# A four-stage-pair transformer on Trainium2: the last four heads of the 8-dimension attentions weigh their values in float32

## The reference, cut to what matters

```
for L in (L0, L2):
    q = layernorm(x) @ Wq (+ bq)              # 128 tokens, 16 heads x 8
    k, v = ctx @ Wk (+ bk), ctx @ Wv (+ bv)   # 77 keys, 16 heads x 8
    p = softmax(q k^T / sqrt(8))              # per head, 128 x 77
    x = x + tanh(gate) * ((p v) @ Wo (+ bo))
```

## Time and profile before

| | |
|---|---|
| runs of the kernel before (us) | 5861.38, 5869.38, 5875.85; median 5869.38 |
| the profiled execution: time, span (us) | 5845.47, 5843.6 |
| mean granted TensorE clock | 0.923 |
| PE, PEld, DVE, ACT, POOL busy (us) | 4882.0, 3691.1, 4188.7, 2757.5, 2105.6 |
| first to last `hiT` work, stage L0 (us) | 28.2 to 568.7 |
| the same, stage L2 (us) | 2493.3 to 3033.8 |
| other big stages, `weigh` products (us) | 935.4 to 1660.6, 3551.2 to 4459.6, 4654.0 to 5367.7 |

### The profile page before, as it was taken

How to read it: one execution, slowest core, us unless ns; L and a number is a source line. 1 busy time by engine, 2 the same in 40 slices (tenths; PEclk the granted TensorE clock), 3 DMA queues, 4 the chain that set the end, 5 groups by cost and what they waited for, 6 DMA issues and landing times. The chain is left out here.

```text
span 5843.6 us, 134152 instructions
## 1 busy us (share of the span) xinstructions
PE 4882.0 (84%) x40251; PEld 3691.1 (63%) x40251; DVE 4188.7 (72%) x10467; ACT 2757.5 (47%) x5756; POOL 2105.6 (36%) x2536
## 2 busy tenths in 40 slices
PE   7888998999942996088879998888888799998898
PEld 5666567888842564066657665777776577776544
DVE  7887775777765332288876767888887699997544
ACT  4554674555520332055555544555554355554344
POOL 3332000011037001643333336777776633333300
PEclk9998998999975998599989998999999899998988
DMA  0000500000011343100000000000000000000000
GB/s 33 2 2 21 230 0 16 5 5 5 5 59 43 131 139 102 48 3 2 2 13 1 0 0 9 0 0 0 0 0 6 7 2 2 2 2 6 1 13 16
DMA packets 113844, 136.89 MB, mean 23 GB/s; under 512 B 45016, under 2 KB 88216, under 8 KB 108956
## 3 DMA queue, kind: packets, MB, share of 16 engines
q1 hardware_dynamic: 105504, 118.30, 6.1%
q0 software_dynamic: 8192, 16.79, 1.0%
HBM read 44.85 MB, written 58.72 MB: 18 GB/s over the span
## 5 line engine op out<-in xcount | busy, mean ns | idle before, releaser
L1881 POOL TENSOR_TENSOR l3a_probs<-l3a_probs,l3a_later 128x512 f32<-128x512 f32 x256 | 320.7, 1283 | 4.9 <-DVE l3a_total L2069 4.9
L1867 POOL TENSOR_TENSOR l3a_keys<-l3a_kT,head 128x2048 f32<-128x2048 f32 x64 | 230.5, 3601 | 232.5 <-ACT l3a_kT L1994 232.5
L1296 POOL DMA_INDIRECT l1c_rows<-l_rows,l1f_slots x128 | 122.2, 955 | 443.8 <-PEq L1288 403.3
L359 POOL TENSOR_TENSOR l0x_keys<-l0x_kT,head 128x1232 f32<-128x1232 f32 x64 | 145.1, 2268 | 354.7 <-ACT l0x_kT L446 354.7
L359 POOL TENSOR_TENSOR l2x_keys<-l2x_kT,head 128x1232 f32<-128x1232 f32 x64 | 145.1, 2267 | 321.1 <-ACT l2x_kT L444 321.1
L1929 PE MATMUL l3a_scores<-l3a_keys,l3a_qT 128*128 128x512 f32 x512 | 256.5, 604 | 4.2 <-POOL l3a_keys L1867 4.2
L166 POOL TENSOR_TENSOR l1x_ve<-l1x_mv,eps 128x1 f32<-128x1 f32 x64 | 12.3, 191 | 656.1 <-DVE l1x_mv L158 656.1
L294 PE MATMUL l3a_po<-l3a_vals,l3a_probsT 128*128 128x32 f32 x2048 | 248.1, 269 | 0.1
L294 PEld LDWEIGHTS l3a_po<-l3a_vals,l3a_probsT 128*128 128x128 f32 x2048 | 247.1, 192 | 0.4 <-ACT l3a_probsT L275 0.4
L250 ACT ACTIVATE l3a_probs<-l3a_probs 128x512 f32<-128x512 f32 x256 | 161.7, 632 | 180.5 <-DVE l3a_probs L241 175.5
L1367 POOL TENSOR_TENSOR l2f_hid<-l2f_prod,l2f_route 128x512 f32<-128x512 f32 x128 | 152.2, 1194 | 255.3 <-DVE l2f_prod L1514 242.2
(11 more groups left out here) (520 smaller groups left out, 17315.5 us busy)
## 6 DMA issues: line engine op xcount, KB each, us to landing
l_rows<-l0f_zeros SPq DMA_DIRECT2D x34, 1024.0 KB, 25.9
l1f_parts<-l1f_split SPq DMA_DIRECT2D x40, 512.0 KB, 3.6
l1e_x_in<-l_rows SPq DMA_DIRECT2D x40, 256.0 KB, 2.8
l1f_down<-l1f_w SPq DMA_DIRECT2D x40, 256.0 KB, 2.4
l_rows<-l1e_y_out SPq DMA_DIRECT2D x40, 256.0 KB, 2.7
l1f_w<-in_L_W SPq DMA_DIRECT2D x16, 256.0 KB, 3.2
out_x<-x_res SPq DMA_DIRECT2D x16, 256.0 KB, 2.0
x_res<-in_x SPq DMA_DIRECT2D x1, 3840.0 KB, 12.6
```

The source lines that it names most:

```text
L359: pool.tensor_tensor(keys[it.par][:, :, :], kT[it.par][:, :].unsqueeze(1).to_broadcast([P, HEADS, KEYS]), g.head8[:, :].unsqueeze(2).to_br ...
L1296: pool.indirect_dma_start(rows[p][:, k * P:(k + 1) * P], None, g.xs[:, :], bass.IndirectOffsetOnAxis(ap=slots[:, it.b * CHOICES + k:it.b * ...
L1867: pool.tensor_tensor(keys[it.par][:, :, :, :], kT[it.par][:, :, :].unsqueeze(2).to_broadcast([P, J, G4, T]), g.head32[:, :].unsqueeze(1).u ...
L1881: pool.tensor_tensor(v, v, later[:, :].unsqueeze(1).to_broadcast([P, 4, T]), ALU.mult).then_inc(s_masked, 1)
```

## The change

For the last chunk (heads 12 to 15) of both 8-dimension stages, the turned probabilities are copied to one float32 buffer `wholeT`, the values of these heads to a float32 `vwhole`, and the product is one float32 matmul a head. The other twelve heads keep their three fp16 products. DVE's remainder 3 is dropped; `vhi` and `vlo` hold twelve heads; ACT makes one more small copy, `vwhole`, which `vlo` waits for; fetch 1 and fetch 3 no longer share a buffer, so fetch 3 waits for `weigh3` of the round before and fetch 1 for `weigh1` of it. Scaling by 64 and 1024 falls away for the four heads in numerator and denominator alike (their ones column holds 1.0).

```diff
@@ Softmax
+        if last_whole:
+            self.wholeT = st.sb("wholeT", [keys, CHUNK * P])
...
+        self.rests = self.nc_ - 1 if last_whole else self.nc_
@@ Softmax.turn
-        if (due := nth(it, self.nc_, c, back=2)) is not None:
+        if self.last_whole:
+            if c == 1:
+                if (due := nth(it, self.nc_, self.nc_ - 1, ago=1)) is not None:
+                    pe.wait_ge(self.s_fetch, due)
+            elif (due := nth(it, self.rests, c - 2 if c >= 2 else self.rests - 1, ago=0 if c >= 2 else 1)) is not None:
+                pe.wait_ge(self.s_rest, due)
+        elif (due := nth(it, self.nc_, c, back=2)) is not None:
             pe.wait_ge(self.s_rest if self.split else self.s_fetch, due)
@@ Softmax.fetch
-        if (due := nth(it, self.nc_, c, back=2)) is not None:
+        if (due := nth(it, self.nc_, c, back=4 if self.last_whole and c % 2 else 2)) is not None:
             act.wait_ge(self.s_values, due)
         src = self.ps_turn[c % 2][0:self.keys, :]
-        if self.split:
+        if self.last_whole and c == self.nc_ - 1:
+            act.copy(self.wholeT[:, :], src).then_inc(self.s_fetch, 1)
+        elif self.split:
@@ Softmax.times_values
-        pe.wait_ge(self.s_rest if self.split else self.s_fetch, nth(it, self.nc_, c))
+        whole = self.last_whole and c == self.nc_ - 1
+        if self.split and not whole:
+            pe.wait_ge(self.s_rest, nth(it, self.rests, c))
+        else:
+            pe.wait_ge(self.s_fetch, nth(it, self.nc_, c))
         for k in range(CHUNK):
             h, cols = CHUNK * c + k, slice(k * P, (k + 1) * P)
+            if whole:
+                last = pe.matmul(out_of(h), self.wholeT[:, cols], values_of(h), start=True, stop=True)
+                continue
@@ small_head_attention
+    SPLITS = HEADS - CHUNK
-        vhi, vlo = st.sb2("vhi", [KEYS, HEADS, D + 1], F16), st.sb2("vlo", [KEYS, HEADS, D + 1], F16)
+        vhi, vlo = st.sb2("vhi", [KEYS, SPLITS, D + 1], F16), st.sb2("vlo", [KEYS, SPLITS, D + 1], F16)
+        vwhole = st.sb2("vwhole", [KEYS, CHUNK, D + 1])
...
+                    pool.memset(vwhole[i][:, :, D:D + 1], 1.0).then_inc(s_ones, 1)
...
+                    if c == 3:
+                        pe.wait_ge(s_vwhole, nth(it))
+                        sm.times_values(pe, it, c, lambda h: o_p[:, h, :], lambda h: vwhole[it.par][:, h - SPLITS, :])
...
-                    act.activation(vhi[it.par][:, :, 0:D], v_heads, ACT.Copy, scale=SPLIT).then_inc(s_vhi, 1)
+                    act.activation(vhi[it.par][:, :, 0:D], v_heads[:, 0:SPLITS, :], ACT.Copy, scale=SPLIT).then_inc(s_vhi, 1)
+                    act.copy(vwhole[it.par][:, :, 0:D], v_heads[:, SPLITS:HEADS, :]).then_inc(s_vwhole, 1)
...
                     dve.wait_ge(s_vhi, nth(it))
+                    dve.wait_ge(s_vwhole, nth(it))
...
-                steps = ... "divide remainder0 remainder1 maximum0 normalize maximum1 shift0 remainder2 remainder3 shift1 statistics values maximum2 add shift2"
+                steps = ... "divide remainder0 remainder1 maximum0 normalize maximum1 shift0 remainder2 shift1 statistics values maximum2 add shift2"
```

More of the change, by code:

```diff
@@ L198, with __init__ @@
 class Softmax:
-    def __init__(self, st, g, banks, heads_of_bank, keys, scale, ps_turn, split=False):
+    def __init__(self, st, g, banks, heads_of_bank, keys, scale, ps_turn, split=False, last_whole=False):
         self.g, self.banks, self.keys, self.scale = g, banks, keys, scale
@@ L211, in __init__ @@
         self.mx, self.probs = st.sb2("mx", [P, HEADS]), st.sb2("probs", [P, HEADS, keys])
-        self.split = split
+        self.split, self.last_whole = split, last_whole
+        if last_whole:
+            self.wholeT = st.sb("wholeT", [keys, CHUNK * P])
         if split:
@@ L324, in small_head_attention @@
         ln = LnFront(st, g, pa[:, 0:P])
-        sm = Softmax(st, g, scores, HELD, KEYS, scale, turned, split=True)
-        s_w, s_ctx, s_ones = st.sem("s_w"), st.sem2("s_ctx"), st.sem("s_ones")
+        sm = Softmax(st, g, scores, HELD, KEYS, scale, turned, split=True, last_whole=True)
+        s_w, s_ctx, s_ones, s_vwhole = st.sem("s_w"), st.sem2("s_ctx"), st.sem("s_ones"), st.sem("s_vwhole")
         s_kv, s_q, s_kT, s_vhi, s_vlo, s_qT, s_keys = [st.sem(n) for n in ("s_kv", "s_q", "s_kT", "s_vhi", "s_vlo", "s_qT", "s_keys")]
@@ L413, in weigh @@
                             pe.wait_ge(s_o, due)
-                        pe.wait_ge(s_ones, 4)
-                    sm.times_values(pe, it, c, lambda h: o_p[:, h, :], lambda h: (vhi[it.par][:, h, :], vlo[it.par][:, h, :]))
+                        pe.wait_ge(s_ones, 6)
+                    if c == 3:
+                        pe.wait_ge(s_vwhole, nth(it))
+                        sm.times_values(pe, it, c, lambda h: o_p[:, h, :], lambda h: vwhole[it.par][:, h - SPLITS, :])
+                    else:
+                        sm.times_values(pe, it, c, lambda h: o_p[:, h, :], lambda h: (vhi[it.par][:, h, :], vlo[it.par][:, h, :]))
                 def turn_o(it):
@@ L505, in value_remainder @@
                     dve.wait_ge(s_vhi, nth(it))
-                    dve.scalar_tensor_tensor(vlo[it.par][:, :, 0:D], v_heads, SPLIT, vhi[it.par][:, :, 0:D],
+                    dve.wait_ge(s_vwhole, nth(it))
+                    dve.scalar_tensor_tensor(vlo[it.par][:, :, 0:D], v_heads[:, 0:SPLITS, :], SPLIT, vhi[it.par][:, :, 0:D],
                                              ALU.mult, ALU.subtract).then_inc(s_vlo, 1)
@@ L519, in _ @@
                          "statistics": (statistics, 0), "normalize": (lambda it: ln.normalize(dve, it), 1),
-                         **numbered("remainder", lambda it, c: sm.remainder(dve, it, c), 4, 3),
+                         **numbered("remainder", lambda it, c: sm.remainder(dve, it, c), 3, 3),
                          "values": (value_remainder, 1), "divide": (divide, 4), "add": (add, 4)}
-                skewed(dve, g.B, in_order(steps, "divide remainder0 remainder1 maximum0 normalize maximum1 shift0 remainder2 remainder3 "
+                skewed(dve, g.B, in_order(steps, "divide remainder0 remainder1 maximum0 normalize maximum1 shift0 remainder2 "
                                                  "shift1 statistics values maximum2 add shift2"), 6)
```

## The result

The changed kernel takes 6047.64 us (median of 4 runs, 6038.97 to 6050.22) against 5868.85 us: ratio 1.0303, 95% interval 1.0291 to 1.0316, so 179 us slower. That is 1.40 us for each of 128 rounds. The forecast had 1.02 us and 6000 us; the time lies inside the range.

What follows compares the result with a forecast made beforehand. It took a loop closing on PE (last `weigh`, `vhi`, `vlo`, `queries`) as the bound. Terms 0.64 + 0.05 + 0.33 = 1.02 us a round, times 128 = +131 us, gave 6000 us as a median; range 5930 to 6090.

Steps and rivals of the forecast that it cites:

- (a): Remainder 3 leaves DVE's queue: 0.66 us less DVE work a round, but 0 on the path.
- DVE bound: Rival: DVE's queue holds the loop at `vlo`, so each round shortens by 0.69 us, to 5781 us; chance 0.03.
- (b): `weigh3` on PE: four float32 products replace twelve fp16 ones, 0.64 us more a round, including 0.07 for the first load.
- Four loads a product: Rival: each float32 product in `weigh3` needs four load-and-product pairs, round 2.08 us longer, 6135 us; chance 0.03.
- cheap float32: Rival: the eight float32 records of `weigh3` flow like fp16 ones, leaving 0.05 us a round, 5876 us; chance 0.03.
- (c): Extra ACT copy `vwhole` behind `vhi`, with `vlo` waiting for it: 0.05 us more a round, bounds 0 and 0.15.
- the wait at turn 2: PE's new waits at turns 0 to 3 ask for things done long before: 0 on the path.
- ACT's idle time before `vhi`: Sign in the profile after: ACT's idle time there grows by about 0.6 us a round.
- (e): PE's clock: a longer thin part from `weigh2` to `queries` brings more half-speed stretches, 0.33 us more a round.
- every round hit: Rival: PE's clock falls in each round, 1.56 us a round more, 6069 us; chance 0.12.
- The price of a hit: Extra length of a round hit by a half-speed stretch: 1.30 us, from rounds of 9.37 and 8.07 us.

Runs made afterwards that it cites:

- e1: The changed kernel with DVE's fourth 77x512 conversion a round kept in its old place, its result unread; ratio 1.0307.
- e2: The kernel before with only the extra small ACT copy (77x32, float32, unread) behind `vhi`, and `vlo` waiting for it; ratio 1.0010.
- e12: The kernel before, all fp16 products kept, with an unread 756-column ACT copy behind `vhi` that `vlo` waits for; ratio 1.0356.
- e7: The changed kernel with `weigh2` and `weigh3` issued before `score2` and `output` on PE; ratio 0.9979.
- e10: The changed kernel with the query projection moved to the first score bank and ACT's second exponential put ahead of `fetch_values`; ratio 1.0005.
- e5: The kernel before with the query projection written to the first score bank, so `queries` need not wait for `vlo`; ratio 0.9834.

## Why the prediction was right, and where it was short

The sign, the range and the path of the added work (`weigh3`, `vhi`, `vlo`, `queries`) held; the sum was 0.38 us a round short, nearly all of it in one term, the clock.

(a), DVE's remainder at 0: right, and shown by e1. The rival of the DVE bound is out.

(b), `weigh3` in float32 at 0.64 us: measured 1.04 - 0.45 = 0.59 us. The length 1.02 was near 1.04. The 0.07 us for a first load that couldn't hide was wrong: the first float32 product starts 0.03 us behind the last fp16 one. Four loads a product is out with the eight records, and cheap float32 with their 1.04 us. The Trainium skill's "FP8 and Floating Point Precision", section TensorE Precision Notes, has four passes for true fp32; the profile shows two records for a product, so the passes don't give the cost of this shape. The load price of "TensorE: Matmul & The Clock Gate", section on LDWEIGHTS (128 / 1.2 = 107 ns for 128 columns, by which the prediction's estimate was 0.65 us), gives 0.58 us once the 0.07 is taken off, and the trace agrees with 0.59: the starts of the eight records lie (1.04 - 0.26) / 7 = 0.11 us apart.

(c), the small copy at 0.05 us: PE's pause grew by 0.08 us in the changed kernel, where `vhi` and `vlo` are a quarter shorter, and in e2, where they are not, the round grew by 0.13. The copy was cheaper than priced (172 ns and not 200), but `vlo` starts 0.10 us after its end, where it started 0.02 us after the end of `vhi`.

(b) and (c) were 0.69 us together; the full-clock round says 0.73. That is partly luck: the measured parts are 0.59 and 0.08, and the wait at turn 2, which the working put at nothing, fills the gap. Of the signs, ACT's idle time before `vhi` grew by more than the 0.6 us that were named: from 0.83 us to 1.71.

(e), the clock at 0.33 us: this is the term that was mis-sized. It measured 0.66. What was off is the share of rounds hit: "I take between one in two and two in three", and it is 36 of 40. The rival "every round hit", with 6069 us and a chance of 0.12, was nearer to 6048 than the forecast.

The price of a hit was wrong too. The 1.30 us between 9.37 and 8.07 hold 0.36 us of the loop's end, which only the hit one of those two rounds has. In the same way the 2.79 us of "about two hits" in six rounds are three loop ends (1.08 us) and two falls (1.71 us); the count of one in three was right. By its own kind of round a hit costs 0.77 to 0.94 us before (9.20 and 9.37 against 8.43) and 1.12 to 1.13 us after (9.92 against 8.80, 10.28 against 9.15). With these prices the share that was forecast gives 0.59 x 1.12 - 0.30 = 0.36 us, near the 0.33 of the sum, so the two errors in the price nearly cancel and the share is what failed. Every round hit would be 1.12 - 0.30 = 0.82 us, near the rival's 0.87, and a few rounds still escape.

The working had weighed against the rival that two of three rounds pass without a fall at a pause of the same kind. They are not of one kind: half of the rounds have no loop end, and none of those is hit before. e12 shows that about 0.75 us more in front of `queries` brings the falls to nearly all rounds. But e2 warns against a rule: 0.13 us more brought fewer.

What stays open: how the number of falls depends on the length of the round and of its thin part. For the short kind of round the runs have 8.07 us (clock 0.93), 8.20 (0.96), 8.80 (0.84) and 8.85 (0.83) with a pause, and 1.00 with the pause filled; e7 (no pause, 0.93) and e10 (a pause elsewhere, 1.00) don't fit a rule by idle time. They give no law. Not tried: a loop body of more than two rounds, which would make the loop ends rarer; more buffers for `vhi` and `vlo`, which would cut the wait for `weigh3` itself; and a place for `values` behind remainder 0 in DVE's order.

## What to carry to other kernels

Before work is moved off a busy engine, look at what it waits for next: an engine at 85% can be late for nobody, and then its relief turns into idle time at its next wait, here 0.60 of 0.66 us. With few moving columns their number doesn't set the price of float32: eight records took 0.98 us with 32 of them, 1.04 with 9 and 1.06 with 4. When a loop closes on PE, a longer step can cost twice, as here: 0.73 us in the loop and 0.66 in more rounds with a half-speed stretch. So compare rounds at full clock and the mean clock apart, and compare like with like: with two rounds in the loop body, every second one was 0.36 us longer at full clock.

## What the runs showed of the hardware

- Six useless matmuls in a pause of 0.8 us made the kernel faster, by 0.6% before and by 1.9% after the change, by lifting the clock's mean from 0.93 and 0.84 to 1.00.
- The clock fell to half in nearly every round although PE was busy 90% of the time (361.45 of 400 us) and never sat idle for a whole microsecond before `queries`.
- A loop 0.13 us longer can bring fewer falls (e2: clock 0.93 to 0.96, rounds hit 16 to 9 of 47).
- PE can be busy 97% of the time (e7, 386.58 of 400 us) with its clock at 0.93, and wait about 1 us in nearly every round (e10) with its clock at 1.00.
- The end of the loop body on PE, with a branch of 0.21 us, makes its round 0.36 us longer (8.43 against 8.07 us) in the kernel before. In e5, with the loop opened, the steady rounds of both kinds take 7.71 us.
- Four float32 products on a 77x128 stationary tile take 1.04 us, twelve fp16 ones on tiles of the same shape 0.45 us.
